# Two batches first in the planned part, rounded rows turned in float32, and a new order of steps

## The reference

```
x += t0 * swiglu_by_token_class(ln(x))      # 4 experts, one per token
x += t4 * moe(ln(x))                        # 64 experts, 4 per token, and 2 shared ones
x += t1 * mlstm(ln(x), ctx)                 # 16 heads; per head h * rsqrt(var(h) + eps) * scale
x += t5 * lora(ln(x))                       # 8 low-rank pairs, the best one per token
x += t2 * attention(ln(x), [ctx, x])        # one head, softmax over 512 columns
x += t6 * bitffn_silu(ln(x))                # rows and weights rounded
x += t3 * topk_attention(ln(x), ctx)        # 54 of 256 scores are kept
x += t7 * bitffn_relu2(ln(x))               # rows and weights rounded
```

## Time and profile before

| what | value |
|---|---|
| median of 3 runs | 607.99 us (606.97 to 608.83) |
| profiled execution | 605.15 us, span from first to last instruction 603.4 us |
| TensorE busy | 468.6 us (78%) |
| VectorE busy | 365.5 us (61%) |
| ScalarE busy | 233.1 us (39%) |
| GpSimd busy | 169.0 us (28%) |
| mean granted TensorE clock | 0.856 of full speed |

### The profile page before, as it was taken

The page is one execution under the profiler, slowest core; times in us unless marked ns, Lnnn a source line. Parts: engine busy times, 40 slices in busy tenths (PEclk is TensorE's granted clock), DMA queues, the critical chain, the costliest instruction groups (busy, mean ns, idle before and its releaser), DMA issues.

```text
span 603.4 us, 7259 instructions
## 1 busy us (share of the span) xinstructions
PE 468.6 (78%) x2562; PEld 337.0 (56%) x2562; DVE 365.5 (61%) x1021; ACT 233.1 (39%) x407; POOL 169.0 (28%) x165
## 2 busy tenths in 40 slices
PE   1999987669999857768997089999966786755664
PEld 0788863228887635445655057688743464533442
DVE  6473367882113364886565344523488999999844
ACT  1200035243243625254533032133548661334775
POOL 4000007783803675440236560100110010000200
PEclk9999978798999957779688559999989987965877
DMA  8960502103994410001000100000000000000000
GB/s 273 263 288 1 190 20 77 36 24 123 343 312 144 143 44 14 7 2 36 2 1 3 68 1 1 0 1 0 1 1 1 0 2 1 2 0 0 18 26 28
DMA packets 25124, 37.59 MB, mean 62 GB/s; under 512 B 5678, under 2 KB 20148, under 8 KB 25088
## 3 DMA queue, kind: packets, MB, share of 16 engines
q1 hardware_dynamic: 22016, 33.38, 16.3%
q0 software_dynamic: 3072, 3.75, 2.1%
HBM read 32.32 MB, written 9.44 MB: 69 GB/s over the span
## 4 chain that ended last, share of the span: by engine, by line
PE 47%; DVE 31%; POOL 9%; ACT 6%; issue 5%; DMA 2%; POOLq 0%; DVEq 0%; ACTq 0%
PE bank L1441 5%; PE bank L1528 5%; PE bank L1451 5%; PE bank L1785 3%; POOL ar L563 3%; PE bank L1550 3%; DVE top L1109 2%; DVE big L1106 2%; DVE HN L612 2%; PE bank L1799 2%; PE bank L1821 2%; DVE bnst L602 2%; PE bank L1862 1%; PE bank L1539 1%; DVE am L989 1%
## 5 line engine op out<-in xcount | busy, mean ns | idle before, releaser
L476 POOL TENSOR_TENSOR rstd<-ve,neghalf 128x2 f32<-128x2 f32 x32 | 25.0, 780 | 258.5 <-DVE ve L607 258.5
L521 POOL DMA_INDIRECT xg_rows<-HN,slot x32 | 31.7, 991 | 21.7 <-DVE slot L733 12.8
L922 DVE TENSOR_TENSOR SH<-bank,HM 128x512 f32<-128x512 f32 x32 | 22.0, 689 | 24.8 <-ACT HM L1284 10.7
L1482 PE MATMUL bank<-HT,SH 128*128 128x512 f32 x64 | 34.8, 705 | 0.0
L780 DVE TENSOR_TENSOR he<-sil,bank 64x64 f32<-64x64 f32 x32 | 7.0, 218 | 45.8 <-ACT sil L1198 45.5
L563 POOL TENSOR_TENSOR ar<-ar,neghalf 128x32 f32<-128x32 f32 x4 | 21.7, 5430 | 39.7 <-DVE ar L886 39.7
L612 DVE TENSOR_SCALAR HN<-X,mv,rstd 128x256 f32<-128x256 f32 x64 | 26.8, 460 | 9.8 <-POOL rstd L476 9.6
L1528 PEld LDWEIGHTS bank<-ph,big 128*128 128x128 f32 x256 | 31.0, 192 | 1.1 <-issue 0.4
L1441 PE MATMUL bank<-HM,CT 128*128 128x256 f32 x128 | 30.6, 403 | 1.2 <-DVE HM L636 1.2
L1284 ACT ACTIVATE HM<-bank 128x512 f32<-128x512 f32 x32 | 19.2, 600 | 30.9 <-PE bank L1637 27.1
L1528 PE MATMUL bank<-ph,big 128*128 128x64 f32 x256 | 30.4, 272 | 0.0
(11 more groups left out here) (351 smaller groups left out, 1173.7 us busy)
## 6 DMA issues: line engine op xcount, KB each, us to landing
big<-in_ew SPq DMA_DIRECT2D x16, 768.0 KB, 7.6
xg_rows<-zer SPq DMA_DIRECT2D x1, 2048.0 KB, 8.5
ph<-xg_rows SPq DMA_DIRECT2D x16, 128.0 KB, 4.6
y_rows<-ph SPq DMA_DIRECT2D x16, 128.0 KB, 3.2
X<-in_x SPq DMA_DIRECT2D x4, 256.0 KB, 6.8
CT<-in_ctxT SPq DMA_DIRECT2D x1, 1024.0 KB, 7.7
CN<-in_ctx SPq DMA_DIRECT2D x1, 1024.0 KB, 11.5
ar<-in_q2g SPq DMA_DIRECT2D x1, 1024.0 KB, 5.1
```

Of the source, the lines that this page charges most:

```text
L476: pool.tensor_tensor(rstd[:, b, :], ve[:, b, :], neghalf[:, 0:TB], ALU.pow)\
L521: pool.indirect_dma_start(out=xg_dram, out_offset=bass.IndirectOffsetOnAxis(slot[:, t, k:k + 1], 0), in_=HN[:, t, :], in_offset=None, boun ...
L922: dve.tensor_tensor(cs[:, g, :], bank[i % 3][:], dcs[:, i % 2, :], ALU.mult).then_inc(s["s_cs"], 1)
L1482: last = pe.matmul(bank[bk + q][:], w[:, k, P * f:P * (f + 1)], HT[:, k, 512 * c:512 * (c + 1)], start=(k == 0), stop=(k == KD - 1))
```

## The change

The planned part now begins with batches 0 and 1 (`LATE = 2`): the end of the head rows of batches 2 and 3 and the turn of their tokens become steps of the planned part (`power`, `headx`, `heads`, `turn1`). `HR` and `vr` get a second buffer (`HR` in `ph`), and `heads_turned` of batches 2 and 3 waits for the first of GpSimd's three operations on the batch two before. The subtraction of MAGIC moves into ScalarE's copies from PSUM: `XQ` and `HQ` are gone, TensorE turns the float32 tiles `HN` and `H`, for hidden rows into both banks of the batch, and ScalarE subtracts with a bias as it copies, in two halves for hidden rows. The Sigmoid and the Exp for `coef` move to the end of the experts (near L1208), and waits move from the start of the planned part to the steps that need them. All four orders are new. They begin:

```diff
 FFN2 = [((name, j), engines) for j in range(TB) for name, engines in
-        (("in2a", "TVS"), ("in2b", "TVS"), ("round2", "VS"), ("turn2", "TS"), ("out2", "TV" if j < TB - 1 else "TVG"))]
+        (("in2a", "TVS"), ("in2b", "TVS"), ("round2", "S"), ("turn2", "TS"), ("out2", "TV" if j < TB - 1 else "TVG"))]
 FFN3 = [((name, j), engines) for j in range(TB) for name, engines in
-        (("in3", "TVS"), ("round3", "VS"), ("turn3", "TS"), ("out3", "TV"))]
-STEPS = ([("heads", "VG"), ("turn1", "TVS"), ("route1", "TVS"), ("low1", "TV"), ("lowturn1", "TS"), ("lowout1", "TVG"),
-          ("norm4", "TVS"), ("keys2", "TS"), ("values2", "TS"), ("scores2", "TVS"), ("probs2", "TS"), ("mix2", "TVG"), ("norm5", "VSG"), ("turn5", "TS")] + FFN2 +
+        (("in3", "TVS"), ("round3", "S"), ("turn3", "TS"), ("out3", "TV"))]
+STEPS = ([("power", "G"), ("headx", "G"), ("heads", "VG"), ("turn1", "TVS"), ("route1", "TVS"), ("low1", "TV"), ("lowturn1", "TS"), ("lowout1", "TVG"),
+          ("norm4", "TVS"), ("keys2", "TS"), ("values2", "TS"), ("scores2", "TVS"), ("probs2", "TS"), ("mix2", "TVG"), ("norm5", "VS"), ("turn5", "TS")] + FFN2 +
          [("norm6", "TVS"), ("queries3", "TS"), ("scores3", "TVS"), ("clip3", "VS"), ("probs3", "TS"), ("mix3", "TS"),
-          ("project3", "TVG"), ("norm7", "VSG"), ("turn7", "TS")] + FFN3)
+          ("project3", "TVG"), ("norm7", "VS"), ("turn7", "TS")] + FFN3)
+
+LATE = 2
 
 TURNS_OF = {
-    "T": ("02101213023013020123020132010312312313002330112201023031031212013203231010302121313002302323"
-          "1110033311202012103130210213232323232"),
-    "V": ("01230312300113220331200310122030132102103201301231203102312130230321310303210120131302120101"
-          "30123232323232"),
-    "S": ("01213023001230201201312312300303102101220132130321032013013212310203023101310102323231310003"
-          "230111201213013021032123232323232"),
-    "G": ("3012300112233012300113322"),
+    "T": ("00101021210200213031132031230122313020310232130130120120132310320212010203311321232323201013"
+          "30312201120333021201032321233031022313"),
+    "V": ("00121200213123033221303011200321213030120123102032112030321231323203101320213302013213203123"),
+    "S": ("00121200031231013021102320102331020313102112032013203120213102302030123211323213210102333201"
+          "0213031302120123230230313120232313"),
+    "G": ("2223031323012301230123"),
 }
 
 
 def plan(engine):
 
-    left = [[step for step, engines in STEPS if engine in engines and (step not in ("heads", "turn1") or b == B - 1)]
+    left = [[step for step, engines in STEPS if engine in engines and (step not in ("power", "headx", "heads", "turn1") or b >= LATE)]
             for b in range(B)]
...
-        HR = ar[:, 0:TB * NH * 17].rearrange("p (j h c) -> p j h c", j=TB, c=17)
-        HRJ = pair(ar[:, 0:TB * NH * 17], TB * NH)
+        heads_of = [ar[:, 0:TB * NH * 17], ph[:, 0:TB * NH * 17]]
+        HR = [m.rearrange("p (j h c) -> p j h c", j=TB, c=17) for m in heads_of]
+        HRJ = [pair(m, TB * NH) for m in heads_of]
...
-        vr = ar[:, 1936:1968]
+        vr = [ar[:, 1936:1968], ar[:, 2000:2032]]
...
-        LAST = [("turn", B + 1), ("heads", 6), ("heads", 7), ("turn", B + 2)]
+        LAST = [("turn", B + 1), ("heads", 6), ("heads", 7)]
...
-        BEFORE = 3 * B + B - 1
+        BEFORE = 3 * B + LATE
...
-            for b in range(B):
+            def head_power(b):
+
                 pool.wait_ge(s["s_v16"], b + 1)
-                pool.tensor_tensor(rs, vr, neghalf[:], ALU.pow).then_inc(s["s_r16"], 1)
+                pool.tensor_tensor(rs, vr[b % 2], neghalf[:], ALU.pow).then_inc(s["s_r16"], 1)
+
+            def head_rows(b):
+
                 pool.wait_ge(s["s_r16"], b + 1)
-                pool.tensor_tensor(hh, HRJ[:, :, 0:DH], rs.unsqueeze(2).broadcast_to([P, TB * NH, DH]), ALU.mult)\
+                pool.tensor_tensor(hh, HRJ[b % 2][:, :, 0:DH], rs.unsqueeze(2).broadcast_to([P, TB * NH, DH]), ALU.mult)\
                     .then_inc(s["s_hh"], 1)
                 pool.wait_ge(s["s_hh"], 3 * b + 1)
                 pool.tensor_tensor(pair(hhf), pair(hhf), lns[:].unsqueeze(1).broadcast_to([P, TB, D]), ALU.mult)\
...
                 pool.wait_ge(s["s_hh"], 3 * b + 2)
                 xs = X[:, TB * b:TB * (b + 1), :]
                 pool.tensor_tensor(xs, xs, pair(hhf), ALU.add).then_inc(s["s_hh"], 1)
-                if b < B - 1:
-                    ln_rstd(b, 3 * B + b + 1)
+
+            for b in range(LATE):
+                head_power(b)
+                head_rows(b)
+                ln_rstd(b, 3 * B + b + 1)
             for step, b in PLAN["G"]:
+                if step == "power":
+                    head_power(b)
+                if step == "headx":
+                    head_rows(b)
                 if step in STATS:
                     ln_rstd(b, BEFORE + nth("V", STATS, step, b))
-                if step in QUANTS:
-                    pool.wait_ge(s["s_xf"], nth("S", QUANTS, step, b))
-                    pool.tensor_scalar(XQ[:, b], HN[:, TB * b:TB * (b + 1), :], -MAGIC, 1.0, ALU.add, ALU.mult)\
-                        .then_inc(s["s_qn"], 1)
...
-                link(dve.tensor_tensor(sq, HRJ[:, :, 0:DH], HRJ[:, :, 0:DH], ALU.mult))
+                rows_in = HRJ[b % 2][:, :, 0:DH]
+                link(dve.tensor_tensor(sq, rows_in, rows_in, ALU.mult))
                 link(dve.tensor_reduce(vs[:], sq, AX.X, ALU.add))
-                dve.scalar_tensor_tensor(out=vr[:], in0=vs[:], scalar=1.0 / DH, in1=e2[:], op0=ALU.mult, op1=ALU.add)\
+                if b >= 2:
+                    dve.wait_ge(s["s_r16"], b - 1)
+                dve.scalar_tensor_tensor(out=vr[b % 2], in0=vs[:], scalar=1.0 / DH, in1=e2[:], op0=ALU.mult, op1=ALU.add)\
                     .then_inc(s["s_v16"], 1)
...
             heads_sum(3)
             heads_var(3)
-            heads_add(2)
-            heads_norm(2)
...
                 if step == "mix2":
+                    dve.wait_ge(s["s_ex2"], nth("S", ["scores2"], "scores2", b))
                     link(dve.reciprocal(sum2[:, b], sum2[:, b]))
...
-                if step in ROUNDS:
-                    dve.wait_ge(s["s_hr"], nth("S", ROUNDS, step, b))
-                    dve.tensor_scalar(HQ[b], H[b], -MAGIC, None, ALU.add).then_inc(s["s_hq"], 1)
...
+            landed(act, "small")
+            act.activation(alpha[:], mix[:, 2:3], ACT.Sigmoid)
             act.preload_act_table_set("natural_log_exp_and_others")
+            act.activation(mix[:, 3:4], mix[:, 3:4], ACT.Exp).then_inc(s["s_mixe"], 1)
...
                 act.wait_ge(s["s_job"], job("heads", TB * b + t) + 1)
-                if b >= 1:
-                    act.wait_ge(s["s_hh"], 3 * b)
-                act.activation(HR[:, t], pair(job_bank("heads", TB * b + t)[:], NH)[:, :, 0:17], ACT.Copy)\
+                if b == 1:
+                    act.wait_ge(s["s_gx"], NT)
+                if b >= 2:
+                    act.wait_ge(s["s_hh"], 3 * (b - 2) + 1)
+                act.activation(HR[b % 2][:, t], pair(job_bank("heads", TB * b + t)[:], NH)[:, :, 0:17], ACT.Copy)\
                     .then_inc(s["s_freea"], 1)
...
             heads_turned(3, 1)
-            tokens_copy(2)
-            act.activation(alpha[:], mix[:, 2:3], ACT.Sigmoid)
-            act.activation(mix[:, 3:4], mix[:, 3:4], ACT.Exp).then_inc(s["s_mixe"], 1)
-            act.wait_ge(s["s_coef"], 1)
             for step, b in PLAN["S"]:
...
                     act.wait_ge(s["s_qt"], nth("T", QTURNS, step, b))
-                    act.activation(XQT[:, b], pair(bank_a(b)[:, 0:S].bitcast(BF16)), ACT.Copy).then_inc(s["s_qc"], 1)
+                    act.activation(XQT[:, b], pair(bank_a(b)[:]), ACT.Identity, bias=magic[:, 1:2])\
+                        .then_inc(s["s_qc"], 1)
...
                 if step in HTURNS:
-                    act.wait_ge(s["s_hqt"], nth("T", HTURNS, step, b))
-                    act.activation(HQT[b], pair(bank_a(b)[:].bitcast(BF16), KI), ACT.Copy).then_inc(s["s_hqc"], 1)
+                    for h in range(2):
+                        act.wait_ge(s["s_hqt"], 2 * nth("T", HTURNS, step, b) - 1 + h)
+                        last = act.activation(HQT[b][:, 4 * h:4 * h + 4, :], pair(bank[2 * b + h][:], 4), ACT.Identity,
+                                              bias=magic[:, 1:2])
+                    last.then_inc(s["s_hqc"], 1)
...
                 if step == "scores3":
+                    act.wait_ge(s["s_coef"], 1)
                     act.wait_ge(s["s_sc3"], nth("T", ["scores3"], step, b))
...
-            tokens_turn(B + 2)
-            landed(pe, "late")
-            pe.wait_ge(s["s_qw"], NQ)
             pe.wait_ge(s["s_freea"], read_before(len(ORDER) - 1)[1])
             for step, b in PLAN["T"]:
...
                 if step == "route1":
-                    if b == B - 1:
+                    if b >= LATE:
                         pe.wait_ge(s["s_ht"], 2 * B + nth("S", TURNS, "turn1", b))
...
```

(16 more changed lines are left out.)

8 lines of the change are left out of this document (3 added, 5 removed).

## The result

| kernel | median us | runs | against the kernel before, 95% |
|---|---|---|---|
| before | 607.48 | 605.03 to 608.83 | |
| changed | 582.31 | 581.59 to 583.24 | 0.9587 (0.9561 to 0.9614) |

The change makes the kernel 25.2 us faster. The profiled execution took 582.46 us (span 580.7), 22.7 less than that of before. The clock's mean rose from 0.856 to 0.891.

The account below looks back on a forecast made before the run. Bound by alternating waits: a GpSimd hole, a TensorE stage, a VectorE stage, a tail. Leads of 24.1 us by the last `clip3` plus 2.7 in the tail make 26.8: 605.15 to 578.4 profiled, 581 median with 2.84 added; range 571 to 597.

Parts of the forecast that it names:

- Start: Start of the planned part: batch 3's wait goes, first `low1` at 338.7 instead of 355.70; TensorE's lead 15.3 us.
- the loop's own end does not move: End of the loop before the planned part: VectorE still waits there for GpSimd's sums of batches 0 and 1.
- GpSimd's margins: GpSimd's late work on batches 2 and 3 is ready 5.9, 1.0 and 1.4 us before it is wanted; nothing charged.
- Rival C: A late GpSimd result holds VectorE in `heads`/2 or `heads`/3 and the 15.3 us lead is lost: 596 us; chance 0.06.
- D: Granted clock stays at 0.5 through the TensorE stage, so its products take twice as long: about 647 us; chance 0.05.
- TensorE stage: Low rank and attention 2: lead kept, table loads cost TensorE 1.6 us; `mix2`/3 ends at 437.1 against 450.77.
- VectorE stretch: From the end of `mix2`/3 to the last `clip3`: 93.3 us instead of 103.7, ending at 530.4.
- 0.4 lost in balance: VectorE's stretch up to the last `clip3`: new waits more than cancel those that go, by 0.4 us; range 0 to 5.
- Eight subtractions as 5.5 us: VectorE's stretch up to the last `clip3` loses eight of 16 rounding-constant subtractions of 0.69 us each: 5.5 us.
- Float32 turns: TensorE's float32 transposes: 0.87 us per eight against 0.44 in bf16, 8.6 us more work, none on the path.
- Tail: From the last `clip3` to the end: 44.1 us instead of 46.8, ScalarE setting the pace with 40.0 of work; gain 2.7.
- Moved Sigmoid and Exp: Moved from the path's start to about 196 us; one more load at most, some 1.7 us, covered by ScalarE's idle time.

Follow-up runs that it names:

- its experiment: The changed kernel with one buffer for the head rows instead of two, its order of steps kept: 588.65 us, 0.9686 against the kernel before.
- without switches: The changed kernel with Identity in place of the feed-forward part's Silu, so that the eight table loads fall away: 575.19 us, 0.9459 against the kernel before.
- The run with the old path: The changed kernel with the old rounding: VectorE and GpSimd subtract the constant again, TensorE transposes in bf16; 591.13 us, 0.9722 against the kernel before.
- taking 3.4 us of work off it: The kernel with `turn2.1`/3 first on ScalarE, plus VectorE copying half of six of the eight turned hidden blocks in the tail: 579.21 us, 0.9546.

## Why the prediction was right, and where not

The forecast was 581 us, and 578.4 for the profiled execution; that took 582.46. By its steps:

- **Start: right, but the end of the loop before it was not.** From VectorE's sum for batch 3 to the score factor 2.94 us were forecast and 2.94 measured (336.35 to 339.29), from there to `low1` 1.57 plus a handoff, and 1.48 measured. The first `low1` came at 340.77 instead of 338.7. TensorE's last turn of heads began 1.7 us later than in the kernel before, which differs from run to run (332.0 to 335.7 in all kernels), and took 0.9 us longer at half clock. The half clock is no scatter: that turn takes 1.94 us in each of the twelve kernels with the new start, and 1.06 in both with the old one. So "the loop's own end does not move" was wrong by 0.9 us; why the clock has fallen there stays open. The second buffer gives 6.2 us of the lead by its experiment.
- **GpSimd's margins: right.** The sums of batch 2 were done 5.2 us before `heads`/2 asked for them (forecast 5.9), and those of batch 3 2.1 us before `heads`/3 did (1.4). `power`/3 ended at 356.3, and GpSimd then waited 1.41 us for the statistics of `lowout1`/0 (1.0). Rival C did not come, nor did D: the clock was at 1.00 by 346.
- **TensorE stage: the end right (437.30, forecast 437.1), its terms not.** That the late start and the shorter stage cancel is luck. Loads were to cost TensorE 1.6 us between 411 and 422. Its waits there are 1.46, but two more follow at 427.5 and 430.4, together 3.3, and without switches the stage is 3.5 us shorter. On the other side the clock rose 3.6 us into `low1`, not 5.7 (the mean of 0.71 in the earlier trace rows makes it 5.9 in the kernel before), which gives back about 1.0. From the first `low1` to 437.30 the stage took 96.5 us, 98.4 were forecast; with 1.9 more for the loads and 1.0 less for the clock, some 2.8 us remain in which it ran faster than I had counted. I had taken the stage as full, but in the kernel before TensorE waits 6.4 us between its first `low1` and the end of `mix2`/3; the two longest waits are these:

```profile
390.94 0.66 PE L1423 MATMUL bank<-identf,HN 128*128 128x128 f32 x4 [1.44 <-DVE HN L612]
...
447.42 1.89 PE L1862 MATMUL bank<-WK,HM 128*128 128x512 bf16 x4 [2.67 <-ACT HM L1374]
```

  In the changed kernel it waits 1.1 us there besides the four waits for loads. How much of the 2.8 us that makes, no run tells.
- **VectorE stretch: the step that failed.** 93.3 us forecast, 97.7 measured (437.30 to 534.99). The term "0.4 lost in balance" for new waits was mis-sized: all of VectorE's waits in the stretch make 6.6 us, 4.3 more than before, and two of them, 1.11 and 2.36 us behind `clip3`/1, make 3.5 of the 4.4. I had not followed ScalarE's queue there, in which a turn's copies stand behind a table load, nor expected the half clock at 490.
- **Eight subtractions as 5.5 us: near only in this order, and in part by luck.** 5.7 in the new one, 1.3 in the old. In the new order seven of them lie in that stretch, 4.8 us, and VectorE's waits are 1.1 us longer with them; in the old order its waits grow by 3.7 us when eight are taken out. A sum of durations was no price here, since the waits move with it.
- **Float32 turns: the duration right, the price not tested alone.** Eight take 1.04 us at full clock (for instance at 447.33), as forecast. The run with the old path takes them out only together with the rest of the new one, and is slower.
- **Tail: right in size (43.4, forecast 44.1); its cause is open.** In the changed kernel ScalarE is busy 39.3 us of the 43.4 (forecast 40.0) and waits 1.7, as it would if it set the pace. Yet taking 3.4 us of work off it left 44.4: ScalarE then waits 6.0 us, most of it for VectorE, which has the new copies in its queue and waits there for TensorE. Whether a chain through all three engines was as long as ScalarE's work from the start, or the copies made it so, no run tells apart.
- **Moved Sigmoid and Exp: right**, nothing.

In the profiled execution the misses are 0.2 at `mix2`/3, +4.4 in the VectorE stretch and -0.7 in the tail: 3.9 of the 4.1 us. The median lies nearer to the forecast than the profile does, since I had added 2.84 us for the distance of the kernel before between the two, and the changed kernel's is nil. That is luck.

Of the table loads the Trainium skill (ScalarE: Activation LUTs, "Table sets: the hidden batching unit") says to batch activations by set. Here the runs agree that switches cost (7.1 us for eight), not that batching pays by itself: putting two Exp together took four loads out and gained nothing (583.52 against 582.31 us), since the Silus that VectorE waits for came later.

## What to carry to other kernels

Taking work off an engine that is busy 92% of a stretch was worth a quarter of its duration (1.3 of 5.5 us) where other engines' results came just in time; test the edit in the order in which it is to stay. In a hand-made order look at each queue for a short copy that others wait for, behind something long whose own result is not yet due: moving one such copy gave 3.2 us. An engine that is nearly full may not be the only one that sets the end: giving a part of its work away gained nothing here, as the engine that took it had to wait for its input in its own queue.
